# Opening order changed, and the second batch's normalised x turned by transfers and block transposes

## The chip, the cores and the metric

One core of one Trainium2 chip runs the whole program. The metric is the device time in microseconds (us), less is better. TensorE, VectorE, ScalarE and GpSimd each work through a queue of their own in order; SyncE issues nearly all transfers. Engines wait for one another only where the code has a semaphore wait.

## What is computed

A transformer block with modulation by a condition (sizes: 2 batches of 512 tokens, width 512, inner width 1376):

```python
mod = (_silu(L0_c) @ L0_wmod).reshape(L0_c.shape[0], 6, 1, -1)
sa, ca, ga, sb, cb, gb = (mod[:, 0], mod[:, 1], mod[:, 2], mod[:, 3], mod[:, 4], mod[:, 5])
ga = (2 * (ga >= 0) - 1) * jnp.maximum(jnp.abs(ga), 0.25)
gb = (2 * (gb >= 0) - 1) * jnp.maximum(jnp.abs(gb), 0.25)
h = _layernorm(x, axis=-1) * (1 + ca) + sa
x = x + ga * _L0_attn_ref(h, L0_attn_weight, L0_attn_mask)   # h @ (weight, masked in blocks of 32x32).T
h = _layernorm(x, axis=-1) * (1 + cb) + sb
x = x + gb * _L0_ffn_ref(h, ...)        # (silu(h@Wg.T*ag) * (h@Wu.T*au)) @ Wd.T * ad
```

## The kernel before

The work is one hand-written order per engine. Tokens come in 8 tiles of 128 (4 for each batch), the width in 4 chunks k of 128, the inner width in 11 chunks c.

**Opening and first linear layer.** VectorE takes the statistics of the first four x tiles (`stats`), normalises them (`normalise`, with the reciprocal deviation from GpSimd's `inverse_deviation`), sums the mask in rows of 32 (`sum_mask`), turns the block sums into a keep pattern (`keep_blocks`) and makes the modulation columns (`mod_columns`). TensorE runs a stretch of warm-up matmuls on the identity, then `rows_ln1` (rows of the modulation), `mask_blocks` (block sums over partitions), `columns_ln1` (rows to columns) and `transposes(n)`, which turns chunk k of four normalised tiles into PSUM. ScalarE copies the rows and does `modulate(n)`: scale and shift while it copies the turned chunk to SBUF. GpSimd multiplies the attention weights by the keep pattern (`mask_weights`). Then TensorE runs `linear(b, k, t)`, 16 products for each batch, and a table `between` says which small steps come after which product.

**Second normalisation.** Sets n = 8 to 11 (first batch) and 12 to 15 (second batch) of `transposes` and `modulate` make the input of the wide layer. For the second batch all of `xn` is normalised in step 2, and one set is turned in each of the steps 6 to 9, into bank 3.

**Wide layer.** 22 steps s (11 chunks for each batch). In step s TensorE does `gate_up(s)`, 16 products of 128 by 512, and `down(s - 2)`, 8 products. ScalarE rounds the weights (`round_gu`, `round_d`) and applies silu; VectorE does `ffn_inner(s)`: a product (line 565), a rounded copy (572) and the rest (574), and for the sets 12 to 15 `split`, a rounded copy and rest of h. The waits that link them: `gate_up(s)` starts when `ffn_inner(s - 2)` has its product (`inner_ok`), `down(s)` when the rest of `ffn_inner(s)` is there.

SyncE's queue, in order: x of the first batch, mask, modulation weights and attention weights by chunk, the rest of x, the gates' weights, then the wide layer's weights; after them it waits for `grow_ok` (step 5), passes the second gate through memory, and later stores the output.

Of the kernel before, what the change touches and what calls it, by code (L numbers as in the profile page):

```python
# [25 lines left out]
ALU = mybir.AluOpType  # L26
# [3 lines left out]
P = 128  # L30
# [10 lines left out]
EPS = 1e-5  # L41
GATE_MIN = 0.25
STEPS = NB * C
WARM_UP = 18
BY_POOL = TT
SETS = KT + 2
BLOCKS = [2, 2, 2, 2, KT, 3 * KT]
# [18 lines left out]
def adaln_block(nc, x, att_w, att_mask, cond, mod_ln1, mod_ln2, mod_gate, w_gu, w_gu_tail, w_down,  # L66
                scales, scales_tail, down_scale, out):
    with ExitStack() as ctx:
# [43 lines left out]
        flags = sb("flags", [1, len(GROUPS)], I32)  # L112

        gates = maskt[:, :, :].bitcast(F32)

        h1 = wffn[:, H1_CHUNK:C, :].rearrange("p c n -> p (c n)")[:, 0:NB * KT * SEQ]\
            .rearrange("p (b k t) -> p b k t", b=NB, k=KT)
# [66 lines left out]
        att_done = sem("att_done")  # L184
        att_read = sem("att_read")
        x1_ok = sem("x1_ok")

        checked = sem("checked")
        flagv_ok = sem("flagv_ok")
# [26 lines left out]
        @block.sync  # L216
        def _(sp):
            for t in range(TT):
                sp.dma_start(xt[:, t, :], x[t * P:(t + 1) * P, :]).then_inc(d_x[t], 16)  # L219

            def load_att(k):
                sp.dma_start(maskt[:, k, :], att_mask[k * P:(k + 1) * P, :]).then_inc(d_mask[k], 16)

                sp.dma_start(modw[:, k // 2, 2 * (k % 2):2 * (k % 2) + 2, :], mod_ln1[k])\
                  .then_inc(d_ln1[k], 16)
                sp.dma_start(awork[:, k, :], att_w[k * P:(k + 1) * P, :]).then_inc(d_att[k], 16)

            def load_x(t):
                sp.dma_start(xt[:, t, :], x[t * P:(t + 1) * P, :]).then_inc(d_x[t], 16)

            for k in range(KT):
                load_att(k)
            for t in range(TT, NB * TT):
                load_x(t)
            sp.dma_start(modw[:, 2, :, :], mod_gate[0]).then_inc(d_gate[0], 16)
            sp.wait_ge(rows_done, 2)
            sp.dma_start(modw[:, 0, :, :], mod_ln2[0]).then_inc(d_ln2[0], 16)
            for c in range(C):
                if c == H1_CHUNK:
                    sp.wait_ge(att_done, NB * TT)  # L240
                if c == 1:
                    sp.wait_ge(rows_done, 4)
                    sp.dma_start(modw[:, 1, :, :], mod_ln2[1]).then_inc(d_ln2[1], 16)
                    sp.wait_ge(rows_done, KT + 1)
                    sp.dma_start(modw[:, 2, :, :], mod_gate[1]).then_inc(d_gate[1], 16)
                if c < C - 1:
                    sp.dma_start(wffn[:, c, 0:2 * D], w_gu[c]).then_inc(d_ffn[c], 16)
                    sp.dma_start(raw_d(c), w_down[c * P:(c + 1) * P, :]).then_inc(d_ffn[c], 16)
                else:
                    sp.wait_ge(tail_zero, 1)  # L250
                    sp.dma_start(wffn[:, c, 0:2 * D].rearrange("p (n i) -> p n i", i=P)[:, :, 0:FT],
                                 w_gu_tail).then_inc(d_ffn[c], 16)
                    sp.dma_start(wffn[0:FT, c, 2 * D:3 * D], w_down[c * P:F, :])\
                      .then_inc(d_ffn[c], 16)
            sp.wait_ge(grow_ok, 1)
            for b in range(NB):
                sp.dma_start(gate_line[b], grow[b * KT:(b + 1) * KT, :]).then_inc(d_line, 16)
            sp.wait_ge(d_line, 16 * NB)
            sp.wait_ge(msum_ok, KT)
            sp.dma_start(gates[:, NB:2 * NB, :].rearrange("p b n -> p (b n)"),  # L260
                         gate_line.rearrange("b k i -> (b k i)").partition_broadcast(P))\
              .then_inc(d_gates, 16)
            for n in range(BY_POOL):
                sp.wait_ge(out_ok, n + 1)
                sp.dma_start(out[n * P:(n + 1) * P, :], xt[:, n, :]).then_inc(d_out, 16)
            sp.wait_ge(d_out, 16 * NB * TT)
# [54 lines left out]
        def _(act):  # L321
# [28 lines left out]
            def modulate(n):  # L350

                q, k = divmod(n, KT)
                layer, b = divmod(q, NB)
                act.wait_ge(xt_done, n + 1)
                act.wait_ge(modc_ok, k + 1 if layer == 0 else KT + 1)
                if q < 2:
                    dst = h1[:, b, k, :]
                else:
                    dst = hbuf[:, n % 2, :]
                    if n >= 10:  # L360
                        act.wait_ge(h_lo, n - 9)
                src = bank[4 + n % 2] if q < 2 else bank[n % 2] if q == 2 else bank[3]
                act.activation(dst, src[:, :], ACT.Identity,  # L363
                               bias=modc[:, layer, k, 2 + b:3 + b],
                               scale=modc[:, layer, k, b:b + 1]).then_inc(h_ok, 1)

# [71 lines left out]
        def _(dve):  # L438
# [21 lines left out]
            def normalise(q, tiles=range(TT)):  # L460
                if q:
                    dve.wait_ge(xt_done, TT * q)
                if q >= 2:
                    dve.wait_ge(x1_ok, TT * (q - 1))
                for t in tiles:
                    if t % 2 == 0:
                        dve.wait_ge(rstd_ok, 2 * q + t // 2 + 1)
                        dve.wait_ge(stats_ok, TT * q + t + 2)
                    dve.tensor_scalar(xn[:, t, :], xt[:, q % NB * TT + t, :], mv[:, q, t, 0:1],  # L469
                                      rstd[:, q, t:t + 1], ALU.subtract, ALU.mult).then_inc(xn_ok, 1)  # L470

            def sum_mask(k):
                dve.wait_ge(d_mask[k], 16)
# [103 lines left out]
            def gate_ffn(b, t):  # L577
                n = b * TT + t
                dve.wait_ge(acc_mm, n + 1)
                dve.wait_ge(d_gates, 16)  # L580
                dve.wait_ge(xt_done, 4 * TT)
                if b:
                    dve.wait_ge(out_ok, TT)
                dve.scalar_tensor_tensor(xn[:, t, :], bank[4 + t][:, :], 2.0, gates[:, 2 + b, :],  # L584
                                         ALU.mult, ALU.mult).then_inc(acc_read, 1)

            for t in range(TT):
                stats(0, t)
            normalise(0, (0, 1))
            sum_mask(0)  # L590
            normalise(0, (2, 3))
            keep_blocks(0)
            mod_columns(0)
            sum_mask(1)
            keep_blocks(1)
            mod_columns(1)
            sum_mask(2)
            keep_blocks(2)
            sum_mask(3)
            mod_columns(2)  # L600
            keep_blocks(3)
            stats(1, 0)
            stats(1, 1)
            mod_columns(3)
            stats(1, 2)
            stats(1, 3)
            normalise(1)
            guard_gate(0)
# [10 lines left out]
            for s in range(STEPS):  # L619
                if s == 0:  # L620
                    for t in range(TT):
                        gate_linear(1, t)
                if s == 4:
                    flag_vector(1)
                    read_flag(1)
                ffn_inner(s)
                if s == 0:
                    stats(3, 0)
                    stats(3, 1)
                if s == 1:  # L630
                    stats(3, 2)
                    stats(3, 3)
                if s == 2:
                    normalise(3)
                if s == 3:
                    guard_gate(1)
                if 6 <= s < 10:
                    split(6 + s)
                if s == C + LAG - 1:
                    for t in range(TT):  # L640
                        gate_ffn(0, t)
# [10 lines left out]
        def _(pe):  # L652
# [36 lines left out]
            def transposes(n):  # L689

                q, k = divmod(n, KT)
                dst = bank[4 + n % 2] if q < 2 else bank[n % 2] if q == 2 else bank[3]
                if k == 0:
                    pe.wait_ge(xn_ok, TT * (q + 1))
                if q == 2 and k < 2:
                    pe.wait_ge(att_read, k + 1)
                elif q == 3:
                    pe.wait_ge(h_ok, n)
                elif n >= 2:
                    pe.wait_ge(h_ok, n - 1)  # L700
                for t in range(TT):
# [165 lines left out]
            pe.wait_ge(ident_ok, 1)  # L867
            for _ in range(WARM_UP):
                pe.matmul(bank[0][:, 0:P], ident[:, :], ident[:, :], start=True, stop=True)
            rows_ln1(0)  # L870
            mask_blocks(0)
            columns_ln1(0)
            transposes(0)
            transposes(1)
# [1 line left out]
            rows_ln1(1)  # L876

            between = {
                (0, 0): [lambda: columns_ln1(1)],
                (0, 2): [lambda: mask_blocks(2), lambda: transposes(2)],  # L880
                (0, 3): [lambda: rows_ln1(2)],
                (1, 0): [lambda: columns_ln1(2)],
                (1, 1): [lambda: mask_blocks(3), lambda: rows_ln1(3)],
                (1, 2): [lambda: transposes(3)],
                (1, 3): [lambda: columns_ln1(3)],
                (2, 3): [gate_rows],
# [37 lines left out]
            for s in range(STEPS):  # L924
# [10 lines left out]
                if s == 5:  # L935
# [1 line left out]
                    pe.transpose(bank[3][0:KT * NB, 0:P],  # L937
                                 gscr[:, 1, :, :].rearrange("p k b -> p (k b)"), ident[:, :])\
                      .then_inc(gate_done, 1)
                if s == 6:  # L940
                    pe.wait_ge(grow_ok, 1)
                if 6 <= s < 10:
                    transposes(6 + s)
            down_last()


# [48 lines left out]
```

## Time and profile before

| | us |
|---|---|
| median of 3 runs | 182.52 (181.76 to 183.66) |
| profiled execution, time | 182.35 |
| profiled execution, span | 180.6 |
| TensorE busy in the span | 171.7 (95%) |
| VectorE busy | 92.9 (51%) |
| ScalarE busy | 82.0 (45%) |
| GpSimd busy | 29.8 (17%) |

The span is what the trace covers; 1.75 us of the execution lie around it. TensorE's busy time counts matmuls that wait in the pipeline, so its share says that it is the engine to look at and not that it runs at its peak. All times in the rows below are from the span's start.

### The profile page before, as it was taken

The numbers are of one execution on the slowest core, as the hardware profiler recorded it, in microseconds if no ns is written. First come the engines' busy times: TensorE is split into PE (matmuls) and PEld (weight loads), VectorE is DVE, ScalarE is ACT, GpSimd is POOL, SyncE is SP. The second block draws the span as 40 slices with busy tenths as digits, with TensorE's granted clock in tenths as the row PEclk, the third lists the DMA queues.
The fourth block names the chain that finished last, engine by engine and source line by source line (L and its number), as shares of the span: only waits on it lengthen the run. The fifth ranks groups of instructions, "written<-read, shape, count | busy, mean of one in ns | idle before, by whom it ended". The sixth has DMA issues, their size and how long they took to land.

```text
span 180.6 us, 2529 instructions
## 1 busy us (share of the span) xinstructions
PE 171.7 (95%) x911; PEld 130.3 (72%) x911; DVE 92.9 (51%) x190; ACT 82.0 (45%) x115; POOL 29.8 (17%) x40
## 2 busy tenths in 40 slices
PE   6669999999999999999999999999999999999991
PEld 6655536665458688788888888888888888888880
DVE  6773463483285798334454645229642234442583
ACT  3022213717979986833356437333355343452200
POOL 1344240292009340000000000003800000000000
PEclk9999999999999999999999999999999999999998
DMA  5999998999208600000200000000410000000023
GB/s 165 329 412 394 420 414 301 401 409 402 86 2 276 206 0 4 0 4 1 120 0 4 0 4 2 4 0 0 178 62 0 4 0 4 0 5 0 4 82 150
DMA packets 9364, 21.88 MB, mean 121 GB/s; under 512 B 2456, under 2 KB 2464, under 8 KB 8832
## 3 DMA queue, kind: packets, MB, share of 16 engines
q1 hardware_dynamic: 8224, 20.52, 30.3%
q10 hardware_dynamic: 1120, 1.07, 1.7%
q8 instruction: 16, 0.26, 0.6%
q14 instruction: 4, 0.03, 0.1%
HBM read 19.48 MB, written 2.10 MB: 120 GB/s over the span
## 4 chain that ended last, share of the span: by engine, by line
PE 86%; ACT 4%; DVE 3%; DMA 3%; issue 2%; SPq 1%; ACTq 0%
PE bank L748 45%; PE bank L802 22%; PE bank L718 12%; PE bank L660 3%; PE bank L702 3%; DMA xt<-in_x 3%; ACT junk L375 3%; DVE xn L469 1%; SPq L219 1%; DVE msum L474 1%; ACT whi_gu L382 1%; PE bank L726 0%; PE bank L674 0%; DVE bns L456 0%; DVE xn L584 0%
## 5 line engine op out<-in xcount | busy, mean ns | idle before, releaser
L748 PE MATMUL bank<-ht,whi_gu 128*128 128x512 f32 x352 | 84.3, 393 | 0.3 <-issue 0.3
L748 PEld LDWEIGHTS bank<-ht,whi_gu 128*128 128x128 f32 x352 | 65.6, 188 | 14.9 <-issue 1.2
L565 DVE SCALAR_TENSOR_TENSOR awork<-bank,scal,awork 128x512 f32<-128x512 f32 x22 | 16.5, 750 | 50.7 <-PE bank L748 47.9
L802 PE MATMUL bank<-whi_dn,in_split 128*128 128x512 f32 x168 | 41.8, 390 | 0.0
L802 PEld LDWEIGHTS bank<-whi_dn,in_split 128*128 128x128 f32 x168 | 31.5, 188 | 6.5
L718 PE MATMUL bank<-awork,wffn 128*128 128x512 f32 x64 | 31.0, 602 | 0.0
L421 ACT ACTIVATE awork<-bank,scal 128x512 f32<-128x512 f32 x22 | 15.2, 689 | 34.0 <-PE bank L748 33.4
L382 ACT ACTIVATE whi_gu<-wffn 128x1024 fp32r<-128x1024 f32 x22 | 23.2, 1055 | 7.3 <-PE bank L748 7.3
L718 PEld LDWEIGHTS bank<-awork,wffn 128*128 128x128 f32 x64 | 10.6, 190 | 8.4 <-issue 7.6
L375 ACT ACTIVATE junk<-wffn 128x1536 uint8<-128x1536 uint16 x11 | 16.3, 1480 | 0.6
L574 DVE TENSOR_TENSOR in_split<-awork,in_split 128x512 fp32r<-128x512 f32 x21 | 15.5, 739 | 0.7
L316 POOL TENSOR_TENSOR xt<-xt,xn 128x512 f32<-128x512 f32 x4 | 5.2, 1338 | 57.0 <-DVE xn L584 57.0
L390 ACT ACTIVATE whi_dn<-wffn 128x512 fp32r<-128x512 f32 x21 | 13.1, 622 | 0.0
L456 DVE BATCH_NORM_STATS2 bns<-xt 128x6 f32<-128x512 f32 x16 | 10.9, 680 | 1.8 <-DMA xt<-in_x 1.1
L363 ACT ACTIVATE hbuf<-bank,modc 128x512 f32<-128x512 f32 x8 | 6.1, 774 | 12.4 <-PE bank L702 11.5
L297 POOL TENSOR_TENSOR xt<-xt,xn 128x512 f32<-128x512 f32 x8 | 10.0, 1288 | 7.8 <-DVE xn L543 7.8
L702 PEld LDWEIGHTS bank<-ident,xn 128*128 128x128 f32 x64 | 7.7, 142 | 4.6 <-issue 3.2
L363 ACT ACTIVATE wffn<-bank,modc 128x512 f32<-128x512 f32 x8 | 6.2, 778 | 9.3 <-DVE modc L498 7.0
L341 ACT ACTIVATE rows<-bank 128x128 f32<-128x128 f32 x6 | 1.7, 278 | 17.4 <-PE bank L660 17.4
L702 PE MATMUL bank<-ident,xn 128*128 128x128 f32 x64 | 9.4, 274 | 0.1
L572 DVE CAST in_split<-awork 128x512 fp32r<-128x512 f32 x21 | 9.0, 429 | 0.7
L660 PE MATMUL bank<-modw,sc 128*32 128x128 f32 x192 | 6.5, 276 | 1.8 <-DMA modw<-in_mod_ln 1.8
(58 smaller groups left out, 93.0 us busy)
## 6 DMA issues: line engine op xcount, KB each, us to landing
wffn<-in_w_gu SPq DMA_DIRECT2D x10, 512.0 KB, 8.3
wffn<-in_w_down SPq DMA_DIRECT2D x10, 256.0 KB, 9.1
xt<-in_x SPq DMA_DIRECT2D x8, 256.0 KB, 7.1
modw<-in_mod_ln SPq DMA_DIRECT2D x4, 512.0 KB, 7.6
modw<-in_mod_gate SPq DMA_DIRECT2D x2, 1024.0 KB, 8.3
modw<-in_mod_ln SPq DMA_DIRECT2D x2, 1024.0 KB, 11.1
maskt<-in_att_mask SPq DMA_DIRECT2D x4, 256.0 KB, 6.9
awork<-in_att_w SPq DMA_DIRECT2D x4, 256.0 KB, 7.6
```

Source lines behind the costliest of these rows:

```text
L363: act.activation(dst, src[:, :], ACT.Identity, bias=modc[:, layer, k, 2 + b:3 + b], scale=modc[:, layer, k, b:b + 1]).then_inc(h_ok, 1)
L375: act.activation(junk[:, :], low, ACT.Copy, accum_out=chk[:, c:c + 1])\
L382: act.activation(whi_gu[:, s % 2, :], wffn[:, s % C, 0:2 * D], ACT.Copy)\
L390: act.activation(whi_d(s), raw_d(s % C), ACT.Copy).then_inc(wd_hi, 1)
L421: act.activation(silu_g[:, s % 2, :], bank[gu_bank(s, 0)][:, :], ACT.Silu, scale=scal[:, s % C, 0:1]).then_inc(silu_ok, 1)
L565: dve.scalar_tensor_tensor(inner[:, s % 2, :], bank[gu_bank(s, 1)][:, :], scal[:, c, 1:2], silu_g[:, s % 2, :], ALU.mult, ALU.mult).then_i ...
L574: dve.tensor_tensor(lo, inner[:, s % 2, :], hi.bitcast(F32), ALU.subtract)\
L660: last = pe.matmul(dst[BLK * j:BLK * (j + 1), 0:P], sc[:, j, i * BLK:(i + 1) * BLK], sources[i // each](j)[:, i % each * P:(i % each + 1) ...
L702: last = pe.transpose(dst[:, t * P:(t + 1) * P], xn[:, t, k * P:(k + 1) * P], ident[:, :])
L718: last = pe.matmul(bank[4 * b + t][:, :], h1[:, b, k, t * P:(t + 1) * P], awork[:, k, :], start=(k == 0), stop=(k == KT - 1))
L748: return pe.matmul(bank[gu_bank(s, u)][:, :], w, h, start=(k == 0 and part == 0), stop=(k == KT - 1 and part == 1))
L802: last = pe.matmul(bank[4 + t][:, :], h, w, start=(c == 0 and part == 0), stop=(c == C - 1 and part == 1))
```

## The change

Three things change. In the opening, VectorE sums the first mask chunk ahead of the first two normalised tiles and makes the first keep pattern between the two pairs of tiles; later sums and keep patterns move against the modulation columns, and the third statistics of the second batch move ahead of the last modulation columns. TensorE does one warm-up product less, has the first mask product ahead of the first modulation rows, and takes another table `between`. In the wide layer, the second batch's sets 12 to 15 are no longer turned on TensorE: `normalise(3)` writes each tile with its 32-column blocks in another order, into a part of `modw` whose data is used up; SyncE issues 16 transfers, each of which moves one group of 32 partitions to another group (32 partitions, 4 tiles, 128 columns); and VectorE turns 32 by 32 blocks with one instruction for each k, behind `ffn_inner` in the steps 5 to 8. `modulate` reads the result from SBUF in place of bank 3.

```diff
-WARM_UP = 18
+WARM_UP = 17
...
+        xq = modw[:, 0, :, :].rearrange("p t (j k c) -> p t j k c", j=P // BLK, k=KT)
+        xb = modw[:, 1, :, :].rearrange("p t (i k c) -> p t i k c", i=P // BLK, k=KT)
...
+            sp.wait_ge(xn_ok, 4 * TT)
+            for j in range(P // BLK):
+                for i in range(P // BLK):
+                    sp.dma_start(modw[BLK * j:BLK * (j + 1), 1, :, i * P:(i + 1) * P],
+                                 modw[BLK * i:BLK * (i + 1), 0, :, j * P:(j + 1) * P]).then_inc(d_blocks[j], 16)
             sp.wait_ge(grow_ok, 1)
...
-                src = bank[4 + n % 2] if q < 2 else bank[n % 2] if q == 2 else bank[3]
-                act.activation(dst, src[:, :], ACT.Identity,
+                src = bank[4 + n % 2][:, :] if q < 2 else bank[n % 2][:, :] if q == 2 else xn[:, k, :]
+                act.activation(dst, src, ACT.Identity,
...
+                if q == 3:
+                    dve.wait_ge(rows_done, SETS)
...
+                    dst, src = xn[:, t, :], xt[:, q % NB * TT + t, :]
+                    if q == 3:
+                        dst = xq[:, t, :, :, :].rearrange("p j k c -> p k j c")
+                        src = src.rearrange("p (k j c) -> p k j c", k=KT, c=BLK)
+                    dve.tensor_scalar(dst, src, mv[:, q, t, 0:1], rstd[:, q, t:t + 1],
+                                      ALU.subtract, ALU.mult).then_inc(xn_ok, 1)
+
+            def transpose_blocks(k):
+                for j in range(P // BLK):
+                    dve.wait_ge(d_blocks[j], 16 * (P // BLK))
+                dve.wait_ge(xt_done, 3 * TT)
+                dve.transpose(xn[:, k, :].rearrange("p (t i c) -> p t i c", t=TT, c=BLK), xb[:, :, :, k, :])\
+                   .then_inc(xt_done, 1)
...
-                dve.wait_ge(xt_done, 4 * TT)
+                dve.wait_ge(h_ok, 4 * TT)
...
+            sum_mask(0)
             normalise(0, (0, 1))
-            sum_mask(0)
+            keep_blocks(0)
             normalise(0, (2, 3))
-            keep_blocks(0)
+            sum_mask(1)
             mod_columns(0)
...
+                if 5 <= s < 9:
+                    transpose_blocks(s - 5)
...
+            mask_blocks(0)
             rows_ln1(0)
-            mask_blocks(0)
...
-                if s == 6:
-                    pe.wait_ge(grow_ok, 1)
-                if 6 <= s < 10:
-                    transposes(6 + s)
```

**VectorE in the opening**, behind the last statistics of the first batch. Lines 469, 474, 479, 486 and 498 of the kernel before (normalise, sum_mask, keep_blocks, the two parts of mod_columns) are lines 485, 497, 502, 509 and 521 of the changed one. Before:

```order
L469 TENSOR_SCALAR xn<-xt,mv,rstd 128x512 [waits stats_ok,rstd_ok]
L469 TENSOR_SCALAR xn<-xt,mv,rstd 128x512
L474 TENSOR_REDUCE msum<-maskt 128x16 [waits d_mask0]
L469 TENSOR_SCALAR xn<-xt,mv,rstd 128x512 [waits stats_ok,rstd_ok]
L469 TENSOR_SCALAR xn<-xt,mv,rstd 128x512
L479 TENSOR_SCALAR keep<-bank 128x16 [waits blk_done]
L486 TENSOR_REDUCE colv<-bank 128x4 [waits cols_done]
L498 TENSOR_TENSOR modc<-colv,oneplus 128x4 [waits consts_ok,cols_ok]
L474 TENSOR_REDUCE msum<-maskt 128x16 [waits d_mask1]
```

And in the changed kernel:

```order
L497 TENSOR_REDUCE msum<-maskt 128x16 [waits d_mask0]
L485 TENSOR_SCALAR xn<-xt,mv,rstd 128x512 [waits stats_ok,rstd_ok]
L485 TENSOR_SCALAR xn<-xt,mv,rstd 128x512
L502 TENSOR_SCALAR keep<-bank 128x16 [waits blk_done]
L485 TENSOR_SCALAR xn<-xt,mv,rstd 128x512 [waits stats_ok,rstd_ok]
L485 TENSOR_SCALAR xn<-xt,mv,rstd 128x512
L497 TENSOR_REDUCE msum<-maskt 128x16 [waits d_mask1]
L509 TENSOR_REDUCE colv<-bank 128x4 [waits cols_done]
L521 TENSOR_TENSOR modc<-colv,oneplus 128x4 [waits consts_ok,cols_ok]
```

The first mask sum moved up by two tiles, the first keep pattern up by two tiles, and the second mask sum ahead of the first modulation columns.

**TensorE in the opening**, from the end of the warm-up (line 869, now 892). Lines 660, 686, 674, 702 and 718 (modulation rows, mask product, columns, transposes, linear) are now 685, 711, 699, 725 and 741. Before:

```order
L869 MATMUL bank<-ident 128x128 x17
L660 MATMUL bank<-modw,sc 32x128 [waits silu_c,d_ln1_0]
L660 MATMUL bank<-modw,sc 32x128 x7
L686 MATMUL bank<-msum,blkones 128x16 [waits consts_ok,msum_ok]
L674 MATMUL bank<-ident,rows 128x128 [waits keep_ok,rows_copied]
L702 MATMUL bank<-ident,xn 128x128 [waits xn_ok]
L702 MATMUL bank<-ident,xn 128x128 x7
L686 MATMUL bank<-msum,blkones 128x16 [waits modc_ok,consts_ok,msum_ok]
```

And in the changed kernel:

```order
L892 MATMUL bank<-ident 128x128 x16
L711 MATMUL bank<-msum,blkones 128x16 [waits consts_ok,msum_ok]
L685 MATMUL bank<-modw,sc 32x128 [waits silu_c,d_ln1_0]
L685 MATMUL bank<-modw,sc 32x128 x7
L699 MATMUL bank<-ident,rows 128x128 [waits keep_ok,rows_copied]
L725 MATMUL bank<-ident,xn 128x128 [waits xn_ok]
L725 MATMUL bank<-ident,xn 128x128 x7
L711 MATMUL bank<-msum,blkones 128x16 [waits modc_ok,consts_ok,msum_ok]
```

The first mask product is now ahead of the first modulation rows; what follows it keeps its order up to the first linear product.

**TensorE in the wide layer**, from the down products of step 9 (line 802, now 825) to the gate and up products of step 10 (line 748, now 771). Of each pair of branches one side runs, the one that reads `whi_dn` and `whi_gu`. Before:

```order
L802 MATMUL bank<-whi_dn,in_split 128x512 x8
L821 UNCONDITIONAL_BRANCH
L702 MATMUL bank<-ident,xn 128x128 [waits h_ok]
L702 MATMUL bank<-ident,xn 128x128 x3
L790 COMPARE_AND_BRANCH [waits inner_ok,wgu_hi]
```

And in the changed kernel:

```order
L825 MATMUL bank<-whi_dn,in_split 128x512 x8
L844 UNCONDITIONAL_BRANCH
L813 COMPARE_AND_BRANCH [waits inner_ok,wgu_hi]
L771 MATMUL bank<-ht,wffn 128x512 x8
L771 MATMUL bank<-ht,wffn 128x512 [waits silu_ok]
```

The four transposes are gone, and the same in the steps 6 to 8.

## Rows read from the trace of the kernel before

**Rows 1.** The page: transfers' share in 40 slices of 4.5 us; the chain by engine.

```profile
DMA  5999998999208600000200000000410000000023
...
PE 86%; ACT 4%; DVE 3%; DMA 3%; issue 2%; SPq 1%; ACTq 0%
```

**Rows 2.** Busy time of each engine in two wide-layer steps, granted clock, transfers.

```profile
101.45:107.38 5.93, 5.93 (x31) 4.90 (x30) 2.99 (x5) 2.94 (x4) 0.00 (x0) 1.00 0.01 3
...
112.95:118.39 5.44, 5.44 (x25) 4.51 (x24) 1.87 (x4) 2.27 (x3) 0.00 (x0) 1.00 0.02 3
```

**Rows 3.** Timeline: step 6 begins; set 12's modulation (start, us, what, idle before).

```profile
83.68 3.92 PE L748 MATMUL bank<-ht,whi_gu 128*128 128x512 f32 x16
...
89.89 0.78 ACT L363 ACTIVATE hbuf<-bank,modc 128x512 f32<-128x512 f32 x1 [2.86 <-PE bank L702]
```

**Rows 4.** Timeline of VectorE in the steps 2, 3, 5 and 6.

```profile
68.41 1.91 DVE L469 TENSOR_SCALAR xn<-xt,mv,rstd 128x512 f32<-128x512 f32 x4
...
70.80 0.75 DVE L565 SCALAR_TENSOR_TENSOR awork<-bank,scal,awork 128x512 f32<-128x512 f32 x1 [0.48 <-PE bank L748]
...
83.28 0.69 DVE L574 TENSOR_TENSOR in_split<-awork,in_split 128x512 fp32r<-128x512 f32 x1
...
87.63 0.75 DVE L565 SCALAR_TENSOR_TENSOR awork<-bank,scal,awork 128x512 f32<-128x512 f32 x1 [3.65 <-PE bank L748]
```

**Rows 5.** Timeline of SyncE: a many-piece transfer's issue, and two small ones.

```profile
55.54 0.62 SPq L251 DMA_DIRECT2D wffn<-in_w_gu_tail  x1
...
84.25 0.60 SPq L257 DMA_DIRECT2D gate_line<-grow  x2
```

**Rows 6.** The page's issues: count, KB each, us from issue to landing.

```profile
wffn<-in_w_gu_tail SPq DMA_DIRECT2D x1, 384.0 KB, 5.9
```

**Rows 7.** Timeline of the opening, 8 to 15 us, all engines.

```profile
8.06 0.99 DVE L469 TENSOR_SCALAR xn<-xt,mv,rstd 128x512 f32<-128x512 f32 x2
...
8.23 0.44 POOL L281 TENSOR_SCALAR veps<-mv 128x2 f32<-128x2 f32 x1 [1.89 <-DVE mv L458]
...
8.97 0.68 DVE L474 TENSOR_REDUCE msum<-maskt 128x16 f32<-128x512 int32 x1
...
9.35 0.65 PE L660 MATMUL bank<-modw,sc 128*32 128x128 f32 x16 [1.79 <-DMA modw<-in_mod_ln]
...
9.66 1.00 DVE L469 TENSOR_SCALAR xn<-xt,mv,rstd 128x512 f32<-128x512 f32 x2
...
10.58 0.17 DVE L479 TENSOR_SCALAR keep<-bank 128x16 f32<-128x16 f32 x1
...
10.89 1.05 POOL L291 TENSOR_TENSOR awork<-awork,keep 128x512 f32<-128x512 f32 x1 [1.27 <-DVE keep L479]
...
11.02 1.04 PE L702 MATMUL bank<-ident,xn 128*128 128x128 f32 x8
...
11.43 0.52 DVE L498 TENSOR_TENSOR modc<-colv,oneplus 128x4 f32<-128x4 f32 x1
...
12.61 0.39 PE L686 MATMUL bank<-msum,blkones 128*128 128x16 f32 x2 [0.55 <-DVE msum L474]
...
13.51 1.13 PE L718 MATMUL bank<-awork,wffn 128*128 128x512 f32 x2
```

**Rows 8.** Line 498 (modc), 11 to 20 us: duration ns min/median/max, first and last start.

```profile
L498 DVE TENSOR_TENSOR modc<-colv,oneplus x3: 163/163/524, 11.4 to 19.9; 128x4 f32<-128x4 f32 x3
```

**Rows 9.** Timeline at 127 us: GpSimd's last two additions of the first batch, and VectorE.

```profile
127.34 2.73 POOL L316 TENSOR_TENSOR xt<-xt,xn 128x512 f32<-128x512 f32 x2
...
128.95 1.67 DVE L574 TENSOR_TENSOR in_split<-awork,in_split 128x512 fp32r<-128x512 f32 x1
```

**Rows 10.** Four mask loads' issues (duration ns, first and last start), landing, us.

```profile
L222 SPq DMA_DIRECT2D maskt<-in_att_mask x4: 432/480/656, 2.6 to 8.1; - x4
...
DMA to landing us min/median/max: 5.1/6.9/7.8
```

**Rows 11.** Warm-up (line 869) by stretches: matmuls, weight loads, granted clock, transfers.

```profile
3.54:4.54 1.00, 1.00 (x7) 1.00 (x6) 1.00 0.95 245
...
5.54:6.54 1.00, 1.00 (x12) 1.00 (x11) 1.00 0.98 277
```

More of the change, by code:

```diff
@@ L186, in adaln_block @@
         x1_ok = sem("x1_ok")
+        d_blocks = [sem(f"d_blocks{j}") for j in range(P // BLK)]
         checked = sem("checked")
@@ L468, in normalise @@
                         dve.wait_ge(stats_ok, TT * q + t + 2)
-                    dve.tensor_scalar(xn[:, t, :], xt[:, q % NB * TT + t, :], mv[:, q, t, 0:1],
-                                      rstd[:, q, t:t + 1], ALU.subtract, ALU.mult).then_inc(xn_ok, 1)
+                    dst, src = xn[:, t, :], xt[:, q % NB * TT + t, :]
[10 more added lines that the diff above has]
+                   .then_inc(xt_done, 1)
             def sum_mask(k):
@@ L588, in _ @@
                 stats(0, t)
+            sum_mask(0)
             normalise(0, (0, 1))
-            sum_mask(0)
+            keep_blocks(0)
             normalise(0, (2, 3))
-            keep_blocks(0)
+            sum_mask(1)
             mod_columns(0)
-            sum_mask(1)
             keep_blocks(1)
+            sum_mask(2)
             mod_columns(1)
-            sum_mask(2)
             keep_blocks(2)
@@ L603, in _ @@
             stats(1, 1)
+            stats(1, 2)
             mod_columns(3)
-            stats(1, 2)
             stats(1, 3)
@@ L691, in transposes @@
                 q, k = divmod(n, KT)
-                dst = bank[4 + n % 2] if q < 2 else bank[n % 2] if q == 2 else bank[3]
+                dst = bank[4 + n % 2] if q < 2 else bank[n % 2]
                 if k == 0:
@@ L696, in transposes @@
                     pe.wait_ge(att_read, k + 1)
-                elif q == 3:
-                    pe.wait_ge(h_ok, n)
                 elif n >= 2:
@@ L878, in _ @@
             between = {
[L879 to L883, printed above, removed]
+                (0, 0): [lambda: columns_ln1(1), lambda: transposes(2)],
+                (0, 1): [lambda: mask_blocks(2)],
+                (0, 2): [lambda: rows_ln1(2)],
+                (0, 3): [lambda: columns_ln1(2)],
+                (1, 0): [lambda: mask_blocks(3)],
+                (1, 1): [lambda: rows_ln1(3)],
                 (1, 2): [lambda: transposes(3)],
```

## The prediction

> **What bounds the kernel now.** I read the page's chain first: 86% of the span is TensorE's [rows 1]. Then the steps of the wide layer one by one: a step with a set of transposes in it takes 5.93 us and one without 5.44, TensorE is busy in all of both, VectorE has 2.99 and ScalarE 2.94 us of work in the first kind [rows 2]. So in the steps 6 to 9 TensorE's own queue is the limit, and what leaves it shortens the step. In the opening it is different: TensorE stands idle 1.79 us ahead of the first modulation rows at 9.35, and again ahead of the second mask product at 12.61, and its first linear product starts at 13.51 [rows 7]. From there on the chain runs through TensorE, and a stretch of ScalarE's weight checks in it (ACT 4% [rows 1]) starts when TensorE has finished the last modulation rows. So a shift of that first linear product is a shift of the end, one for one.
>
> **The transposes that go.** Sixteen transposes leave TensorE in four sets. The step with a set is 5.93 - 5.44 = 0.49 us longer than the one without [rows 2], four times 1.96. The starts say the same: step 6 begins at 83.68 [rows 3] and step 11 at 112.95 [rows 2], 29.27 us for five steps; at 5.44 each they would be 27.20, so 2.07 for the four sets, of which about 0.1 belongs to where the first matmul behind a transpose is drawn. I take 1.96. Nothing else is late in these steps: ScalarE's modulation of set 12 waits for the transpose today, and runs at 89.89 after 2.86 us idle [rows 3].
>
> **What comes in their place on VectorE.** The four tiles of `normalise(3)` take 1.91 us in step 2, from 68.41, and VectorE idles 0.48 ahead of its next product at 70.80 [rows 4]. They now write 32-column pieces. If that costs nothing, they end at 70.3. If each tile falls to the pace of the two-input operation of the same size, 0.69 [rows 4], they end 0.8 later and that product starts 0.3 late; its readers are `gate_up(5)` and `down(3)`, both two steps on. Both ends cost TensorE nothing.
>
> The block transposes have no row in this trace. Nearest are operations on 512 columns at 0.69 to 0.75 us [rows 4]; I take 0.7, with 0.4 (a piece of the 1.91) and twice 0.75 as ends. They stand behind `ffn_inner` in the steps 5 to 8. In step 5 VectorE has nothing from 83.97 to 87.63 [rows 4]; in the steps 6 to 8 its 2.99 us become 3.7, at the far end 4.5, of 5.44. Hidden at both ends. The Trainium skill ("Vector Engine (DVE) Microarchitecture Reference", the reshape front-end) says that a block transpose sustains one element per cycle and lane; no row here shows it, and an estimate from it would leave the sum as it is.
>
> **The sixteen transfers.** They wait for the last normalised tile (70.3 us, or 71.1) at a time when the transfer engines are idle (slices 16 to 18) [rows 1]. One issue costs between 0.30 (two small ones in 0.60) and 0.62 (a transfer of many short pieces) [rows 5], so all are issued after 4.8 to 9.9 us. I take 0.4, near the small ones since each has only 128 pieces: issued at 76.7. Landing after issue: at most the 5.9 us of the short-piece transfer, which has six times the bytes [rows 6]. So they land between 77 and 87.0, likeliest near 79.5. VectorE first asks at 83.97 (it would do nothing else until 87.63), so even the far end costs TensorE nothing. Queued behind them on SyncE is the second gate's path, whose first transfer goes at 84.25 [rows 5] and which is used in step 12, at 124 us: no cost.
>
> **The opening.** Here the order matters. The first mask chunk has landed at 2.57 + 5.1 = 7.7 [rows 10], so VectorE can sum it at once where it now normalises, 8.06 to 8.74 (0.68 long) [rows 7]. TensorE is idle then, and the mask product (0.39) is done by 9.2, with the modulation rows still at 9.35, when their data lands. The first two tiles run 8.75 to 9.75, the keep pattern starts 0.92 after the pair's start as it does now (9.66 to 10.58), ends at 9.84, and GpSimd's `mask_weights(0)` starts 0.14 later, at 9.98, in place of 10.89 [rows 7]. (Its weights, fetched as the third load of the chunk, landed about then.) VectorE's second pair starts at 9.76, so GpSimd's 1.05 us now fall on these two tiles and no longer behind them.
>
> What that does, the trace shows on three rows. The 4-column `modc` at 11.43 took 0.52 us where its like take 0.163 [rows 8], and ended when GpSimd's operation ended, 10.89 + 1.05 = 11.94 [rows 7]. The 574 operation at 128.95 took 1.67 in place of 0.69 while GpSimd's addition ran to 130.07 [rows 9]. And GpSimd's tiny operation at 8.23, which came in the middle of the first tile of a pair, ended at 8.67, behind the first tile (8.60) and not behind the second (9.05) [rows 7]: the one that waits goes first when a tile ends. So I expect GpSimd to come in between the tiles 2 and 3, at 10.2, hold VectorE for about 0.9 (10.89 to about 11.8 was the hold on `modc`), and tile 3 to end at 11.6 in place of 10.76. The Trainium skill states this as a rule ("SBUF — State Buffer", who interferes with whom): VectorE and GpSimd share a pair of ports as an exclusive lock for the whole instruction, and which operations take it. The trace agrees so far as the rows above go; no row has a large GpSimd operation between two normalised tiles.
>
> From there: TensorE's two sets of transposes (1.04) at 11.65 to 12.69; the second mask sum 11.5 to 12.2, columns and `modc` to 12.56 (0.17 and 0.16, unblocked, since GpSimd is done by then); the second mask product at 12.69; and the first linear product 0.90 behind it, as today (12.61 to 13.51) [rows 7], at 13.59. `modulate(0)` runs 12.66 to 13.44 and doesn't bind. That is 0.08 later than now. The rest of the new table `between` only moves the same small steps among the same products, each wait long fulfilled: I take nothing for it, with 0.1 either way. The warm-up product that goes (0.2 us) ends in idle time.
>
> **Sum.** Against the profiled execution: 182.35 - 1.96 + 0.08 = 180.5 us. That execution stands 0.17 under the median of the runs, which themselves spread over 1.9 us; I give 180.5.
>
> **Rivals.**
> 1. *The two tiles keep VectorE, and GpSimd waits.* Then tile 3 ends at 10.76, transposes run 10.8 to 11.9, the second mask sum 10.7 to 11.4, and `modc` waits for GpSimd's end at about 11.7. The mask product follows at 11.9, the second modulation rows are held by their landing near 12.0 and end at 12.8, and the linear product starts there: 0.75 earlier. For it: the two tiles of a pair are drawn overlapping (0.99 for two). Against it: the row at 8.23. Time 182.35 - 1.96 - 0.75 = 179.6.
> 2. *The transposes' 0.49 was not all TensorE's own.* If some other hand-over (weights' loads behind the branch, ScalarE's rounding) holds a step once the set is gone, half comes back: 181.5. Against it: the steps without a set already run at 5.44 with the same hand-overs.
> 3. *TensorE's clock falls in the opening.* In the warm-up 7 matmuls pass in the us from 3.54 and 12 in the us from 5.54 [rows 11], so it starts at the lower of its two levels (1.2 GHz) and is at 2.4 GHz by the second; the granted clock reads 1.00 all through and doesn't show it. Today it stays up over 1.79 us idle. In the changed kernel it has only one short transpose between 10.0 and 11.65. If it fell there, some 1.5 us of small work ahead of the linear layer would double, and the first 3 us of the linear layer would do the work of 1.5: 3.0 us, 182.35 - 1.88 + 3.0 = 183.5.
> 4. *The block transfers land late, and the kernel is slower.* VectorE works in order: behind the transpose in step 5 stands `ffn_inner(6)`, and `gate_up(8)` waits for that one's product. That gate product would start at 94.5 (101.45 less one step of 5.93 is 95.5 now, less two sets), so a landing up to 94.5 - 0.75 - 0.7 = 93.05 is free, each us behind it is lost, and past 95.0 the kernel is slower than before. It takes 24.7 us for sixteen, 1.5 us each, one after the other. At 1.8 each: landing 99.1, 6.0 us lost, 186.5. Against it: 0.62 for the worst issue, and idle transfer engines.
>
> **How the numbers follow.** Forecast 0.52, rival 1 0.27, rival 2 0.09, rival 3 0.07, rival 4 0.03, rest 0.02. The likeliest gives 180.5. Below it the range goes to rival 1's 179.6 with the runs' scatter (half a per cent), 179.0; above, past rival 2 to 182.0; what is left out is rival 3 and 4 and scatter, under 2 in 10. One per cent (1.8 us) is about what a measurement of this kernel can tell from no change. The forecast lies at 1.1% faster, so 0.58 of it counts as faster by over 1%, of rival 1 (1.6%) 0.9: 0.30 + 0.24, with a little of rival 2, 0.56. Slower by over 1% is rival 4 and the bad end of rival 3, 0.04. The rest is within 1%.
>
> **What the profile after would show.** Right: all wide-layer steps from 6 on 5.44 long; one normalised tile of 1.3 to 1.5 us near 10.2 beside GpSimd's `mask_weights`; first linear product near 13.6; block transposes of 0.7 in VectorE's idle time with no wait. Wrong: both tiles at 0.54 and the linear product near 12.8 (rival 1); steps of over 5.5 (rival 2); linear products of twice the length after 13 us (rival 3); VectorE idle in step 5 until a transfer (rival 4). What would break the forecast altogether is a wait in the opening that I take as long fulfilled, above all the third statistics of the second batch, which now stand ahead of the last modulation columns.

## The result and the profile after

The changed kernel takes 180.38 us (median of 4, 180.29 to 180.65), the kernel before 182.46 in the same runs: a ratio of 0.9895, 95% interval 0.9851 to 0.994. The forecast was 180.5. The profiled execution took 180.65, with a span of 178.5 (before 182.35 and 180.6). Two executions further down, 294.27 us of e1 and 183.52 us of e6, ran in a slower state and are left out of the ratios.

The opening, timeline of the changed kernel, all engines (columns as in [rows 7]):

```profile
6.79 0.69 DVE L466 BATCH_NORM_STATS2 bns<-xt 128x6 f32<-128x512 f32 x1 [0.62 <-DMA xt<-in_x]
...
7.62 0.65 DVE L497 TENSOR_REDUCE msum<-maskt 128x16 f32<-128x512 int32 x1
...
8.19 0.99 DVE L485 TENSOR_SCALAR xn<-xt,mv,rstd 128x512 f32<-128x512 f32 x2
...
9.10 0.17 DVE L502 TENSOR_SCALAR keep<-bank 128x16 f32<-128x16 f32 x1
9.18 1.72 DVE L485 TENSOR_SCALAR xn<-xt,mv,rstd 128x512 f32<-128x512 f32 x2
...
9.41 1.21 POOL L301 TENSOR_TENSOR awork<-awork,keep 128x512 f32<-128x512 f32 x1 [0.60 <-DVE keep L502]
...
10.96 1.09 PE L725 MATMUL bank<-ident,xn 128*128 128x128 f32 x8 [0.93 <-DVE xn L485]
...
11.62 0.16 DVE L521 TENSOR_TENSOR modc<-colv,oneplus 128x4 f32<-128x4 f32 x1
...
11.92 0.37 PE L711 MATMUL bank<-msum,blkones 128*128 128x16 f32 x2
...
12.79 1.12 PE L741 MATMUL bank<-awork,wffn 128*128 128x512 f32 x2
```

By single tiles (line 485 up to 12 us: ns min/median/max, first and last start):

```profile
L485 DVE TENSOR_SCALAR xn<-xt,mv,rstd x4: 535/538/1270, 8.2 to 9.6; 128x512 f32<-128x512 f32 x4
```

The second pair of tiles takes 1.72 us in place of 1.00 [rows 7], and one tile of it 1.27 by itself, beside GpSimd's masking of 1.21 in place of 1.05; `modc` is back at 0.16 from 0.52. The first linear product stands at 12.79, 0.72 earlier than before, but the last x tile's statistics began at 6.79 where they began at 7.23. Counted from there, the stretch is 6.00 us in place of 6.28 (and 6.01 and 6.00 in e4 and e12 below, whose opening is the same).

The wide layer: three steps (6, 8 and 11), with the columns of [rows 2], and VectorE, SyncE and TensorE around the block transposes:

```profile
83.08:88.64 5.56, 5.56 (x26) 4.59 (x25) 2.46 (x5) 4.16 (x6) 0.00 (x0) 1.00 0.30 98
...
94.08:99.52 5.44, 5.44 (x25) 4.50 (x24) 3.50 (x7) 2.94 (x4) 0.00 (x0) 1.00 0.01 3
...
110.40:115.84 5.44, 5.44 (x25) 4.51 (x24) 1.87 (x4) 2.27 (x3) 0.00 (x0) 1.00 0.01 3
```

```profile
67.84 1.91 DVE L485 TENSOR_SCALAR modw<-xt,mv,rstd 128x512 f32<-128x512 f32 x4
...
69.78 10.77 SPq L263 DMA_DIRECT2D modw<-modw  x16
...
82.69 0.69 DVE L597 TENSOR_TENSOR in_split<-awork,in_split 128x512 fp32r<-128x512 f32 x1
...
83.08 3.92 PE L771 MATMUL bank<-ht,whi_gu 128*128 128x512 f32 x16
83.30 0.71 DVE L492 STREAM_TRANSPOSE xn<-modw 128x512 f32<-128x512 f32 x1
...
94.08 3.79 PE L771 MATMUL bank<-ht,whi_gu 128*128 128x512 f32 x16
```

The steps 7 to 10 now take 5.44 us each, as long as a step that never had a set of transposes; step 6 takes 5.56. From step 6 at 83.08 to step 11 at 110.40 it is 27.32 us in place of 29.27: 1.95 less. From step 6 to the last addition it is 91.76 us in place of 93.71, and 91.76 to 91.82 in the traces of all ten kernels below that have the block transfers where they are used in time (all but e1 and e4); e1, with the old wide layer, has 93.74. Along the whole span, the changed kernel is ahead by 0.72 at the first linear product, 0.60 at step 6, 2.55 at step 11 and at the last addition (174.84 in place of 177.39), and 2.1 in the span, since the last store landed 0.45 later behind that addition.

### The profile page after: what moved, and what is told of

Read it like the earlier page. It is cut to its first block, busy times and chain, and to the rows that moved or that the text cites. A ratio compares the mean times of both kernels' runs of the same rounds, so it can differ in the third digit from the quotient of the medians.

```text
span 178.5 us, 2520 instructions
## 1 busy us (share of the span) xinstructions
PE 170.8 (96%) x893; PEld 129.6 (73%) x893; DVE 95.1 (53%) x194; ACT 82.0 (46%) x115; POOL 29.6 (17%) x40
## 4 chain that ended last, share of the span: by engine, by line
PE 86%; ACT 4%; DVE 3%; DMA 3%; issue 2%; SPq 1%; ACTq 0%
PE bank L771 45%; PE bank L825 23%; PE bank L741 12%; PE bank L685 3%; ACT junk L385 3%; PE bank L725 3%; DMA xt<-in_x 3%; DVE xn L485 1%; SPq L224 1%; ACT whi_gu L392 1%; PE bank L749 0%; DVE bns L466 0%; DVE xn L607 0%; DVE xt L672 0%; ACT hbuf L373 0%
## 5 line engine op out<-in xcount | busy, mean ns | idle before, releaser
L725 PEld LDWEIGHTS bank<-ident,xn 128*128 128x128 f32 x48 | 5.6, 140 | 5.5 <-issue 3.5
L892 PE MATMUL bank<-ident 128*128 128x128 f32 x34 | 7.0, 400 | 1.5 <-POOL ident L284 1.5
L725 PE MATMUL bank<-ident,xn 128*128 128x128 f32 x48 | 7.0, 275 | 1.0 <-DVE xn L485 0.9
L892 PEld LDWEIGHTS bank<-ident 128*128 128x128 f32 x34 | 6.8, 311 | 1.5 <-POOL ident L284 1.5
```

The source lines that it names most:

```text
L725: last = pe.transpose(dst[:, t * P:(t + 1) * P], xn[:, t, k * P:(k + 1) * P], ident[:, :])
```

## The experiments

Each kernel is timed beside the kernel before; the first four, the next four and the last four each share their runs of it (medians 182.14, 181.91, 182.11).

| kernel | median (range) | ratio (95%) |
|---|---|---|
| e1 opening only | 182.17 (181.46 to 183.61, and one of 294.27) | 0.9983 (0.9947 to 1.0019) |
| e2 wide layer only | 180.86 (180.24 to 182.88) | 0.9929 (0.9895 to 0.9964) |
| e3 later masking | 179.85 (179.50 to 181.37) | 0.9870 (0.9817 to 0.9922) |
| e4 extra transfers ahead | 184.10 (182.96 to 185.49) | 1.0101 (1.0042 to 1.0160) |
| e5 changed again | 180.53 (179.63 to 181.56) | 0.9921 (0.9893 to 0.9949) |
| e6 later masking again | 180.33 (179.49 to 183.52) | 0.9916 (0.9893 to 0.9939) |
| e7 filled, later masking | 179.99 (179.41 to 180.21) | 0.9898 (0.9877 to 0.9919) |
| e8 short warm-up | 181.78 (181.04 to 182.41) | 0.9992 (0.9973 to 1.0011) |
| e9 wide layer only, filled | 180.36 (180.03 to 180.81) | 0.9901 (0.9868 to 0.9934) |
| e10 changed, filled | 180.19 (180.03 to 180.64) | 0.9896 (0.9864 to 0.9929) |
| e11 filled, later masking again | 180.05 (179.06 to 180.22) | 0.9877 (0.9841 to 0.9913) |
| e12 extra transfers behind | 179.82 (179.58 to 180.38) | 0.9877 (0.9839 to 0.9914) |

**e1 and e2, one part each.** The diff is that of e1 against the kernel before. In e1 the pieces `xq`, `transpose_blocks` and the transfers are taken out; in e2 `WARM_UP`, the two orders and `between` are those of before.

```diff
-WARM_UP = 18
+WARM_UP = 17
...
+            sum_mask(0)
             normalise(0, (0, 1))
-            sum_mask(0)
+            keep_blocks(0)
             normalise(0, (2, 3))
...
```

> The opening of the changed kernel (VectorE's and TensorE's order, 17 warm-up products) with the wide layer of the kernel before, TensorE turning the sets 12 to 15 again. In the changed kernel's trace the first linear product came 0.72 us earlier, but the last x tile had landed 0.44 us earlier as well. Theory A (most of the 0.72 was the landing, the order gives 0.28): 0.1 to 0.4 us faster than the kernel before, 182.1 to 182.3, and from the last statistics' start to the first linear product about 6.0 us in place of 6.28. Rival B (the order gives all of it): 0.7 us faster, about 181.7. Rival C (what the prediction said, nothing): 182.5.

> The opening of the kernel before (order, 18 warm-up products) with the changed wide layer: block transfers and VectorE's block transposes. Theory A: all 1.96 us of the transposes come back and nothing else moves, 180.5; steps of 5.44 us from step 7 on. Rival B: part of the gain belongs to the opening, 181.1.

The opening alone gives 0.3 us with an interval from 1.0 less to 0.3 more, so it can't be told from nothing. The wide layer alone gives 1.3, less than 1.96, with executions spread over 2.6 us. A reason for the spread stands in both traces. TensorE in e2, by stretches: busy time and matmuls, granted clock, transfers:

```profile
9.00:11.00 2.00, 1.23 (x21) 1.00 1.03 409
11.00:13.00 2.00, 1.94 (x14) 0.56 1.03 412
13.00:15.00 2.00, 2.00 (x19) 0.50 1.06 405
15.00:17.00 2.00, 2.00 (x5) 0.50 1.03 390
17.00:19.00 2.00, 2.00 (x7) 0.74 1.08 398
```

The granted clock falls to 0.50, the level of 1.2 GHz, at about 11 us, and the stretch to some 18 us runs at half pace (to some 15 us in e1). This execution took 182.88, where e2's lowest took 180.24. The mean granted clock of a whole execution shows such a fall too: it is 0.991 or less in five of e2's twelve, which took 181.72 or more, and 0.995 or more in the others, which took 180.93 or less. The kernel before isn't spared: of its 23 executions measured beside e1 to e4, five have a mean of 0.985 to 0.991 and took 183.31 to 184.02, and the other 18 took 182.65 or less. So e2 measured the wide layer and this fall together, and the expectation of 180.5 was neither met nor refuted by it. The 1.95 stand on the steps' length in the traces. In e1's own trace the fall covers the stretch that was to be 6.00 us, so theory A rests there on the traces of the changed kernel, e4 and e12.

**e3, GpSimd's first masking later.**

```diff
                 pool.wait_ge(keep_ok, k + 1)
+                if k == 0:
+                    pool.wait_ge(xn_ok, TT)
```

> The changed kernel, with one more wait: GpSimd's first weight masking starts only when all four normalised tiles of the first batch are done. Theory A (GpSimd holds the ports between the tiles 2 and 3 and that is on the path): the second pair of tiles takes 1.00 us in place of 1.72, the first linear product comes 0.5 to 0.7 earlier relative to the last statistics, total 179.7 to 179.9. Rival B (the second chunk's mask and modulation weights, which land near 10.6 and 11.5, hold what follows): pair at 1.00 but the linear product at most 0.2 earlier, total 180.2 to 180.4. Rival C (the long pair has another cause): pair stays at 1.7.

Timeline of e3, VectorE and GpSimd, and TensorE:

```profile
9.13 0.99 DVE L487 TENSOR_SCALAR xn<-xt,mv,rstd 128x512 f32<-128x512 f32 x2
...
10.84 0.53 DVE L523 TENSOR_TENSOR modc<-colv,oneplus 128x4 f32<-128x4 f32 x1
...
10.30 1.05 POOL L303 TENSOR_TENSOR awork<-awork,keep 128x512 f32<-128x512 f32 x1 [1.54 <-DVE xn L487]
...
11.52 0.37 PE L713 MATMUL bank<-msum,blkones 128*128 128x16 f32 x2 [0.24 <-DVE modc L523]
...
12.39 1.13 PE L743 MATMUL bank<-awork,wffn 128*128 128x512 f32 x2
```

The pair of tiles is back at 0.99: GpSimd between the tiles was what held it (rival C falls). But now the masking meets `modc`, which takes 0.53 again and lets TensorE's mask product wait. From the last statistics (6.74) to the first linear product it is 5.65 us in place of 6.00. So 0.35 of the 0.73 us of hold come back, and 0.36 move to `modc`. That puts it between theory A and B. The median of 179.85 lies in A's range, but the same kernel once more took 180.33 (e6), so the medians don't decide it; the traces repeat, with 5.63 us in e6 and 5.61 in e11.

**e4 and e12, sixteen more transfers, ahead of the real ones or behind.**

```diff
+            for j in range(P // BLK):
+                for i in range(P // BLK):
+                    sp.dma_start(modw[BLK * j:BLK * (j + 1), 2, :, i * P:(i + 1) * P],
+                                 modw[BLK * i:BLK * (i + 1), 0, :, j * P:(j + 1) * P]).then_inc(d_extra, 16)
```

> The changed kernel, with sixteen more transfers of the same shape (to the third, unused part of modw) issued ahead of the sixteen real ones. The result is the same. At 0.67 us each the real ones land near 69.8 + 21.5 + 2 = 93.3 in place of 82.5, and VectorE waits in step 5 from 83.4 on. Theory A (the prediction's rival 4: only the product of ffn_inner(6) matters, a landing up to about 93 is free): 0 to 0.4 us slower than the changed kernel, 180.4 to 180.8. Theory B (ScalarE works in order too: its modulation of set 12 waits for the turned set, and behind it stands the rounding of step 8's weights, so gate_up(8) starts 0.7 + 0.8 + 1.06 + 0.1 behind the landing, at 96.0 in place of 94.1): 1.9 us slower, about 182.3.

> The changed kernel with sixteen more transfers issued behind the sixteen real ones, so that nothing in the wide layer waits for them; only the second gate's path on the same queue comes later (from 91.6 in place of 83.6, used at 122). Theory A (in the run with the extra ones ahead, all of the loss came from the late landing): the time of the changed kernel, 180.3 to 180.6. Rival (sixteen more transfers cost something by themselves, ahead or behind, in or outside the span): about 1 to 1.8 us over it.

Timeline of e4 around the landing:

```profile
93.23 0.71 DVE L498 STREAM_TRANSPOSE xn<-modw 128x512 f32<-128x512 f32 x1 [10.32 <-DMA modw<-modw]
...
93.98 0.81 ACT L379 ACTIVATE hbuf<-xn,modc 128x512 f32<-128x512 f32 x1 [8.03 <-DVE xn L498]
...
94.70 1.04 ACT L398 ACTIVATE whi_gu<-wffn 128x1024 fp32r<-128x1024 f32 x1
...
96.05 3.92 PE L777 MATMUL bank<-ht,whi_gu 128*128 128x512 f32 x16 [2.27 <-ACT whi_gu L398]
```

With ten more us of wait VectorE's own work did not hold TensorE; ScalarE's did. `modulate(12)` stands ahead of the rounding of step 8's weights, and TensorE waited 2.27 us for that rounding. Theory B holds, and rival 4 of the prediction had the wrong path: a landing is free up to about 91.4 (94.08 less 0.7, 0.8, 1.06 and 0.1), not 93. Behind the real ones, the same sixteen cost nothing: e12 took 179.82, even less than the expected 180.3 to 180.6. The median of e4 is some 3.6 us over the changed kernel's, where the traced execution lost 2.44 in that step (7.88 us from step 7 to step 8 in place of 5.44). The clock is part of the rest: three of the six executions have a mean granted clock of 0.990 or 0.991 and took 183.91 to 185.49, the three others 182.96 to 184.28. In two of these others 3.0 us lie around the span in place of about 2, and why stays open.

**e5 to e8, the clock in the opening.** e5 is the changed kernel, e6 is e3 once more. e7 adds to e6 products in TensorE's idle time, e8 takes warm-up away from the changed kernel; the two diffs are theirs, in this order.

```diff
-WARM_UP = 17
+WARM_UP = 21
...
             rows_ln1(0)
+            for _ in range(2):
+                pe.matmul(bank[0][:, 0:P], ident[:, :], ident[:, :], start=True, stop=True)
             columns_ln1(0)
```

```diff
-WARM_UP = 17
+WARM_UP = 9
```

> The changed kernel as it is, as the measure for the three that follow. In the two runs of single parts (opening only, wide layer only) the profiled executions showed a granted clock of 0.50 between about 11 and 17 us and took 183.6 and 182.9 in place of about 182 and 180.5, so some executions of this one should show it too: 180.3 for most, and a few near 182.5. If none of its executions is over 181, the changed order as a whole is safe from it.

> The changed kernel with GpSimd's first weight masking behind the four normalised tiles, beside the changed kernel of the same job. Theory A (0.4 to 0.6 us of the opening come from GpSimd holding the ports between the tiles 2 and 3): 0.4 to 0.6 us under the changed kernel. Rival (what was seen in the first run was scatter between jobs): equal within 0.2.

> The kernel with the later masking, and TensorE's idle time in the opening filled: 21 warm-up products in place of 17 (about 0.9 us more, ending where the first mask product is due) and two more behind the first modulation rows, into a bank that the first linear product starts anew. Theory A (TensorE's clock falls in the opening of some executions because it stands idle there): the fastest execution stays, the ones over 181 vanish, median 179.7 to 179.9. Rival B (idle time has nothing to do with it): the same share of slow executions as the kernel without filling. If the products are in the way, all are 0.2 to 0.4 slower.

> The changed kernel with 9 warm-up products in place of 17, so that TensorE stands idle from about 4.7 us to the mask product near 8.5. Theory A (the clock in the opening follows from how busy TensorE was before): many executions run 11 to 17 us at the lower level, median 182 to 183. Rival B (17 products or 9 make no difference, the level rises by itself once the linear products run): 180.4.

The changed kernel isn't spared. TensorE in e5, the same stretches:

```profile
9.00:11.00 2.00, 0.76 (x17) 1.00 1.02 406
11.00:13.00 2.00, 1.94 (x14) 0.63 1.04 415
13.00:15.00 2.00, 2.00 (x18) 0.52 1.07 410
15.00:17.00 2.00, 2.00 (x12) 1.00 1.03 386
```

and in the changed kernel's first trace:

```profile
9.00:11.00 2.00, 0.67 (x14) 1.00 1.01 402
11.00:13.00 2.00, 2.00 (x27) 1.00 1.04 414
```

It is the same program: 181.56 us with the fall and 180.65 without. The last addition of e5 stands at 176.43, 1.59 later than at 174.84, with the last statistics 0.10 later; so the fall costs about 1.5 us here. The expectation was a few executions near 182.5; three of seven had the fall and took 181.11 to 181.56. In e2, where the clock stayed down for about twice as long, the fall costs about 2.6 us: the linear layer's run of eight products begins 18.94 us behind the last statistics, in the kernel before 16.31. In e8 the clock is at 0.50 from about 8 us to nearly 15, and all executions are above e5's median of 180.53: theory A, though the median of 181.78 is a little under the 182 to 183 expected. Four of its twelve show no such fall in their mean clock (0.995 to 0.997) and still took 181.04 to 181.41; why stays open. e6 is 0.2 under e5, at the edge of the rival's range and within the scatter of both. e7 has no execution over 180.21, as theory A has it, with a median of 179.99, just over the range.

**e9 to e11, filled kernels.** e9 is e2 with 24 warm-up products and four more behind the first mask product; e10 is the changed kernel with 21, two behind the rows and three behind the columns; e11 is e7 again.

> The changed wide layer with the opening order of the kernel before, and TensorE's idle time there filled: 24 warm-up products in place of 18, and four more behind the first mask product. Theory A (the wide layer gives 1.96 us, and the falling clock had eaten part of it in the run of this part alone): 1.8 to 2.1 us under the kernel before, no execution above 181. Rival (the part gives only the 1.3 us seen): 1.3 under.

> The changed kernel with the idle time filled (21 warm-up products, two more behind the first modulation rows, three behind the first columns), without the later masking. Theory A: like the one above less 0.2 to 0.4 for the order of the opening, that is 2.1 to 2.4 us under the kernel before, no execution above 181. Rival (the order gives nothing): equal to the one above.

> The filled kernel with the later masking once more, beside the two others of this job. Theory A (GpSimd's hold on the ports costs 0.35 us of the opening): 0.2 to 0.4 under the changed kernel filled. Rival (the hold moves from the tiles to the modulation columns and costs the same there): equal within 0.15.

Of the 24 executions of the four filled kernels (e7, e9, e10, e11) none is above 180.81, and none has a mean granted clock under 0.995. Of the 29 of the unfilled ones with the changed opening and wide layer whose transfers are not delayed (the first four, e3, e5, e6, e12) five are above 181. But 18 of the 24 were measured beside e12, which isn't filled and had none above 181 either. Among kernels measured together only e7 (none of 6) against e5 and e6 (four of 14) tells something, and drawn blindly all four would fall on the unfilled side in 21 cases of 100. So that filling keeps the clock up is likely from this and from e8, and not shown.

With no fall in it the wide layer alone gives 1.75 us (e9), just under the 1.8 to 2.1 expected. Its trace shows the six extra products in the way: the first modulation rows start at 9.79 in place of 9.35, and from the last statistics to the first linear product it is 7.06 us in place of 6.28. In e10 this stretch is 6.76 in place of 6.00. e10 is 1.9 under the kernel before, a miss against 2.1 to 2.4, and 0.2 under e9; e11 is 0.1 under e10, which is the rival's "equal within 0.15". Both differences are under what the medians of these runs resolve. Nor do they show that filling gains time: e12 (179.82) and e3 (179.85), both unfilled, have the lowest medians, with e7 and e11 at 179.99 and 180.05.

## Why the prediction was right, step by step

- **The transposes that go, 1.96 us**: 1.95 in the trace, with the steps 7 to 10 at 5.44 and step 6 at 5.56. Rival 2 falls.
- **VectorE's part at nothing**: a block transpose takes 0.71 us (taken 0.7), the four rearranged tiles 1.91 as before [rows 4]. A step with one has 3.50 us of VectorE work. The first came out as taken, the second at its favourable end.
- **The sixteen transfers**: a term outside its bounds, like that of the new table further down. An issue took 0.60 to 1.01 us, 10.77 for all, where I took 0.4 and had 0.62 as the end, from a transfer of many short pieces [rows 5]. Landing is 2.0 us after issue in the median, so the last landed near 82.5 and not 79.5, 0.8 ahead of the use at 83.3. What was wrong is the choice of the value near the small transfers; it cost nothing because 91.4 was the point from which it counts (e4). Rival 4's own point, 93.05, was wrong too: it followed VectorE alone and left out ScalarE.
- **The opening, 0.08 later**: 0.28 earlier, counted from the last statistics. The 6.00 us stand in three traces, the 6.28 only in the one of the kernel before. The mechanism is the one foretold, GpSimd between the tiles 2 and 3 and VectorE held for 0.73 us; e3, which moves GpSimd's operation, takes the hold away. No semaphore wait stands between the two operations, so engines can hold each other without one. The Trainium skill ("SBUF — State Buffer", who interferes with whom) states that such operations exclude each other for the whole instruction. The trace agrees in the order and only roughly in the length: the held tile ends at 10.90, 0.28 behind the end drawn for GpSimd's operation (10.62), where a free tile takes 0.54. The terms were each a little long: the first tile starts 0.57 behind the mask sum and not 0.69, the pair takes 1.72 and not 1.84, and the mask product starts 0.96 behind the transposes and not 1.04. Rival 1 falls by the 1.72; its other sign, a linear product near 12.8, came true only because the x tile landed 0.44 earlier in this execution.
- **The new table `between`, at nothing, with 0.1 either way**: it costs 0.15 us. From the first linear product to the run of eight products it is 10.18 us in the changed kernel (10.17 in e3, e4, e6, e7, e10, e11 and e12) and 10.03 in the kernel before and in e9, which has the old table. So of the opening's 0.28 about 0.13 are left.
- **Rival 3, the clock**: it was put at 0.07 and as a matter of the changed order. It happens in single executions of the changed kernel, of the opening alone, of the wide layer with the old opening and of the kernel before (six of the 52 measured beside the experiments have a mean granted clock of 0.991 or less), and costs 1.5 us (e5) to 2.6 (e2), where 3.0 was taken. None of the changed kernel's first four executions had it. It didn't decide the sign, but it is what the scatter of the runs is made of in part.
- **The total**: forecast 1.88 less in the profiled execution; its span is 2.10 less: 0.44 from the x tile that landed earlier in this execution, 0.28 from the order in the opening, 1.95 from the wide layer, less 0.12 lost between the first linear product and step 6 and 0.45 at the last store. The 0.44 and the 0.45 are of single executions (from the last addition to the end of the span it is 3.66 us here, 3.21 before and 3.13 to 3.21 in all other traces). Around the span 0.4 came back, and a part of that is no accident: 1.75 to 1.85 us lie around the span in all 52 executions of the kernel before and 1.76 to 1.87 in e1, while the medians of the eleven other kernels and of the changed one's first runs are 1.86 to 2.16. So the new wide layer costs about 0.25 us outside the span, a term the prediction didn't have; what it is made of stays open. Added up from the parts that repeat, the change gives 1.95 + 0.28 - 0.15 - 0.25 = 1.83 us, an estimate; the medians gave 2.08 in the first runs and 1.38 in e5. That the forecast of 180.5 came within 0.12 of the measured 180.38 is in part luck: the opening was taken 0.36 too late, and the table and the cost outside the span, 0.4 together, were not counted.

## What to carry to other kernels

Work taken off the engine that bounds a stretch comes back in full inside the span when the steps beside it, with the same hand-overs and without that work, are already shorter by it; read that from two neighbouring windows first. Compare the time outside the span as well, since what replaces the work can cost something there. Before moving a GpSimd operation, look at what VectorE does in the same microsecond: a hold that is moved away from one instruction tends to meet the next. And for a slack, follow every engine that waits in order behind the late result, not only the one that receives it.

## What the runs showed of the hardware

A plain transfer inside SBUF of 32 partitions, 4 by 512 bytes each, takes SyncE 0.60 us to issue, where a mask load of 256 KB takes 0.43 to 0.66 [rows 10], and lands 2.0 us later in the median (3.8 for the slowest of sixteen). TensorE's granted clock fell to 0.50 in the opening of three of the nine traced executions that had 17 or 18 warm-up products and nothing in the idle time (e1, e2, e5). In the two us ahead of it, from 9 to 11 us, TensorE had worked for 0.76 to 1.23 us where the clock fell, and for 0.66 to 1.48 where it didn't, so these figures alone don't tell which execution falls. Further back the two kinds differ: in the three that fell the warm-up had ended at 7.08 to 7.24 us, and from 7 to 11 us TensorE worked for 1.42 to 1.54 us; in the six others the warm-up ended at 7.30 to 8.53, the same products having taken longer, and the busy time was 1.64 to 3.40. With nine traces of kernels that differ, that is an observation and no rule.
